# Transforms once per two steps, the first image's load in two parts, and ScalarE's second norm in another order, in a fused FFT-mixer and patch-attention kernel

## What is computed

```python
def block0(x):                       # channels 16, hidden 32
    h  = pw(ln(x), w_te)             # norm over channels, pointwise product
    F  = fft2(h, axes=(1, 2))
    fc = gelu(pw([real(F), imag(F)], w_fc))
    sp = real(ifft2(re + 1j * im))
    x1 = x + pw(sp, w_tp)
    h2 = pw(ln(x1), w_fe)            # the second norm
    d  = gelu(depthwise3x3(h2) + b_dw)
    return x1 + pw(d, w_fp)          # x2

def block1(x2):                      # hidden 192 = q, k, v of 64 each
    hidden = ln(x2) @ w_hidden       # the third norm
    q, k, v = split(conv3x3(hidden, w_qkv), 3)
    out = irfft2(rfft2(patches8x8(q)) * rfft2(patches8x8(k)))
    out = v * ln(out)                # norm over 64 channels
    return out @ w_out + x2
```

## Time and profile before

| what | us |
|---|---|
| runs | 236.47, 236.66, 239.24 (median 236.66) |
| the profiled execution | 237.58 |
| its span in the trace | 235.8 |
| busy in it: TensorE | 219.5 |
| busy in it: VectorE | 159.4 |
| busy in it: ScalarE | 133.8 |
| busy in it: GpSimd | 76.9 |

### The profile page before, as it was taken

How to read it: one execution, slowest core, us unless ns; L and a number is a source line. 1 busy time by engine, 2 the same in 40 slices (tenths; PEclk the granted TensorE clock), 3 DMA queues, 4 the chain that set the end, 5 groups by cost and what they waited for, 6 DMA issues and landing times.

```text
span 235.8 us, 4977 instructions
## 1 busy us (share of the span) xinstructions
PE 219.5 (93%) x1926; PEld 144.1 (61%) x1926; DVE 159.4 (68%) x301; ACT 133.8 (57%) x286; POOL 76.9 (33%) x70
## 2 busy tenths in 40 slices
PE   7989999895989899779999999999999999999983
PEld 3359434772447557268676676767676777767561
DVE  3995123567743983646489978678786889677793
ACT  3366475323174754344678666667667576766533
POOL 1635500012300000000051766426654364549730
PEclk9999999999799999999999999999999999999999
DMA  6920000000000018989997479999950000000001
GB/s 215 329 70 7 16 8 4 20 3 0 4 0 0 0 64 190 223 193 194 201 197 151 141 137 191 182 179 202 191 118 0 3 24 25 0 1 3 22 0 67
DMA packets 22647, 21.07 MB, mean 89 GB/s; under 512 B 1898, under 2 KB 21242, under 8 KB 22522
## 3 DMA queue, kind: packets, MB, share of 16 engines
q1 hardware_dynamic: 22352, 20.62, 43.0%
q10 hardware_dynamic: 272, 0.14, 0.3%
HBM read 16.58 MB, written 4.02 MB: 87 GB/s over the span
## 4 chain that ended last, share of the span: by engine, by line
PE 68%; DVE 16%; ACT 6%; DMA 6%; issue 2%; SPq 1%; DVEq 0%; ACTq 0%
PE psum L1229 22%; PE psum L1240 13%; PE psum L1250 7%; PE psum L1102 5%; PE psum L1175 4%; PE psum L1260 3%; DMA arena<-parts 3%; DVE xc L781 2%; PE psum L1080 2%; DVE sq L793 2%; PE psum L1090 2%; PE psum L1063 2%; DMA parts<-tr 2%; DVE st L787 2%; PE psum L1286 2%
## 5 line engine op out<-in xcount | busy, mean ns | idle before, releaser
L1229 PE MATMUL psum<-wc,tile 128*128 128x192 f32 (+1 forms) x384 | 59.4, 305 | 3.5 <-ACT tile L378 1.9
L1229 PEld LDWEIGHTS psum<-wc,tile 128*128 128x128 f32 (+1 forms) x384 | 51.4, 159 | 13.7 <-issue 7.8
L557 POOL TENSOR_TENSOR zp<-zp,ln 128x512 f32<-128x512 f32 x14 | 17.8, 1274 | 100.6 <-DVE zp L937 100.6
L916 DVE TENSOR_TENSOR arena<-psum,arena 128x512 f32<-128x512 f32 x32 | 22.1, 691 | 27.5 <-ACT arena L716 27.2
L378 DVE COPY tile<-arena 128x256 f32<-128x256 f32 x64 | 25.1, 435 | 2.1 <-DMA arena<-parts 2.1
L1175 PE MATMUL psum<-arena,wdw 102*128 102x512 f32 x48 | 23.5, 631 | 0.9 <-ACT arena L339 0.9
L716 ACT COPY arena<-psum 128x512 f32<-128x512 f32 x32 | 18.8, 586 | 9.0 <-PE psum L1240 9.0
L1250 PE MATMUL psum<-arena,km 128*64 128x256 f32 x128 | 20.9, 405 | 0.2 <-DVE arena L916 0.2
L709 ACT COPY spec<-psum 128x768 f32<-128x768 f32 x16 | 12.8, 799 | 12.7 <-PE psum L1229 12.7
L558 POOL TENSOR_TENSOR zp<-zp,ln 128x512 f32<-128x512 f32 x14 | 17.8, 1271 | 1.1
L1240 PE MATMUL psum<-spec,km 64*128 64x256 f32 x128 | 18.2, 402 | 0.0
(11 more groups left out here) (129 smaller groups left out, 373.1 us busy)
## 6 DMA issues: line engine op xcount, KB each, us to landing
arena<-padded SPq DMA_DIRECT2D x16, 393.0 KB, 9.8
arena<-parts SPq DMA_DIRECT2D x16, 196.5 KB, 9.7
arena<-padded SPq DMA_DIRECT2D x8, 262.0 KB, 10.4
parts<-tr SPq DMA_DIRECT2D x12, 115.5 KB
wq<-w_qkv SPq DMA_DIRECT2D x1, 1296.0 KB, 11.9
padded<-tr SPq DMA_DIRECT2D x4, 264.0 KB, 3.9
arena<-parts SPq DMA_DIRECT2D x8, 131.0 KB, 9.6
out<-xt SPq DMA_DIRECT2D x8, 128.0 KB, 1.7
```

The lines of the kernel that those rows point to most:

```text
L557: pool_link(pool.tensor_tensor(y, y, along(0), ALU.mult))
L916: dve.tensor_tensor(pr[:, m % 2], f_half(m, 0), kh[:, m % 2], ALU.mult).then_inc(prod, 1)
L1229: last = mm(bank[a][:, HID * h:HID * h + HID], stationary[:, n % 2, 2 * h + a, :], moving[:, :], start=first and h == 0, stop=not first, s ...
```

## The change

Three parts.

**ScalarE's second norm.** In group 0 the root of the first half (`deviation`) now comes before the square of the second half. In group 1 each window copy is followed by one square, both roots and the Gelu table come next, and the last two window copies stand behind the table. The rows are ScalarE's, from the copies of the inverse transform (line 652 before, 664 now) to the first Gelus (line 677 before, 692 now). Lines 588 and 593 are the square and the root before, 593 and 598 now; 339 is the window copy and 582, now 587, the table. Before:

The diff's core:

```diff
+            if n == 0:
+                engine.wait_ge(im_first, 16 * CHUNK_LOADS)
+            elif n == 2:
+                engine.wait_ge(im_ld[0][0], 16 * CHUNK_LOADS)
...
-            store_padded(0)
+            for b in range(2):
+                store_padded(b)
             store_parts(0)
-            load_chunk(0, 0, 0)
-            store_padded(1)
-            store_parts(1)
+            for p, done in enumerate((im_first, im_ld[0][0])):
+                load_taps(0, 2 * p, 2 * p + 2, done)
+                load_last(0, 2 * p, 2 * p + 2, done)
             sp_.wait_ge(fp_mm, 8)
...
+            deviation(1, 0, (0,))
             square(1, 0, (1,))
-            deviation(1, 0)
+            deviation(1, 0, (1,))
...
+                        store_parts(0, LANES[1:])
+                    if j == 7:
+                        store_parts(1, LANES)
...
-            for n in range(32):
+            for s in range(16):
+                gather9(2 * s + 1)
+                if s >= 2:
+                    o_square(s - 2)
+                conv_out(2 * s)
+                if s == 0:
+                    deviation(2, 1)
+                if s >= 1:
+                    k_out(s - 1)
+                if s in (1, 2):
+                    for b2 in range(2):
+                        part(1, s - 1, b2)
+                if s < 15:
+                    gather9(2 * s + 2)
+                if s >= 2:
+                    root(s - 2)
+                u = unit_after(s - 4)
+                if u is not None:
+                    unit_out(u)
+                conv_out(2 * s + 1)
+                if 3 <= s < 15:
+                    turned(s - 3)
...
+            def product(i):
+                dve.wait_ge(k_ev, i + 1)
+                dve.wait_ge(f_mm, i + 1)
+                if i >= 1:
+                    dve.wait_ge(o_mm, i)
+                dve.tensor_tensor(pr, psum[:, 1024:2048], kh, ALU.mult).then_inc(prod, 1)
...
+            for s in range(16):
+                gather(2 * s + 1)
+                if s == 1:
+                    bordered(1)
+                if s >= 2:
+                    o_sum(s - 2)
+                    o_centre(s - 2)
+                if s == 0:
+                    variance(2, 1)
+                if s < 15:
+                    gather(2 * s + 2)
...
-            keep_warm(5, km, 2)
+            keep_warm(4, km, 2)
...
+            def forward(i):
+                pe.wait_ge(qkv_ev, 2 * i + 2)
+                pe.wait_ge(x2_done, 8)
+                if i >= 1:
+                    pe.wait_ge(prod, i)
+                for part, name, signal in ((1, "fk", fk_mm), (0, "fq", f_mm)):
...
+            for s in range(16):
+                conv(2 * s)
+                if s >= 1:
+                    forward(s - 1)
+                u = unit_after(s - 4)
+                if u is not None:
+                    unit(u)
+                if s == 1:
+                    channel_major(1)
+                conv(2 * s + 1)
+                if 3 <= s < 15:
+                    turn(s - 3)
+                if s >= 1:
+                    inverse(s - 1)
...
-            keep_warm(2, km, 3)
+            keep_warm(1, km, 3)
```

More of the change, by code:

```diff
@@ L685, in _ @@
                 square(2, g, (1,))
[L686 removed]
+                if g == 0:
+                    deviation(2, 0)
             def gather9(n):
@@ L1257, in turn @@
                     pe.wait_ge(yt_ev, i)
+                    if unit_after(i - 1) is not None:
+                        pe.wait_ge(pj_ev, unit_after(i - 1) + 1)
                 pe.wait_ge(gated, i + 1)
@@ L1287, in unit @@
                 last.then_inc(pj_mm, 1)
-            for n in range(32):
-                conv(n)
-                if n >= 1:
-                    forward(n - 1)
-                if n == 1:
-                    pe.wait_ge(x2_done, 8)
-                    channel_major(1)
-                if n >= 2:
-                    inverse(n - 2)
-                if n % 2 == 1 and 7 <= n < 31:
-                    turn((n - 7) // 2)
-                u = unit_after((n - 8) // 2)
-                if n % 2 == 0 and u is not None:
-                    unit(u)
-            forward(31)
+            for s in range(16):
+                conv(2 * s)
+                if s >= 1:
+                    forward(s - 1)
+                u = unit_after(s - 4)
+                if u is not None:
+                    unit(u)
+                if s == 1:
+                    channel_major(1)
+                conv(2 * s + 1)
+                if 3 <= s < 15:
+                    turn(s - 3)
+                if s >= 1:
+                    inverse(s - 1)
+            for e in range(2):
+                forward_half(e)
             turn(12)
-            inverse(30)
-            inverse(31)
+            for e in range(2):
+                inverse_half(e)
             turn(13)
```

178 lines of the change are left out of this document (86 added, 92 removed).

## The result

The changed kernel took 241.01 us in the median of four runs (239.38 to 242.86), beside 237.29 for the kernel before. The ratio is 1.016, with a 95% interval of 1.010 to 1.022. It is slower, clear of noise, though by less than the 2% from which the prediction counts a kernel as slower; 232.2 was forecast, and 228.5 to 239 as the range.

What follows compares the result with a forecast made beforehand. TensorE's work was taken to bound the loop, with DMA rates limiting the loads before it. Conv 4 at 110.95 plus the pairs gave loop end 215.1, 4.5 us saved: 232.2 from the 236.66 median, range 228.5 to 239.

Steps and rivals of the forecast that it cites:

- The ring in pairs with a finish: Loop: chain of waits from product to product, through finish and gather; 7.5 us a pair, under TensorE's 7.65.
- the likeliest case: Whole kernel: only the gather is held up by GpSimd's gate, not finish; 232.2 us, chance 0.45 with the no-gain norm rival.
- its two rivals: Loop: finish and gather held up by GpSimd together once (233.7 us, chance 0.23) or one after the other (239.2, 0.12).
- held up twice: Loop, five pairs with a finish: GpSimd delays finish, then the gather again; 9.2 us a turn, 239.2 in all, chance 0.12.
- pairs without a finish: Loop: the gather, held up beside GpSimd's product, makes the chain of waits 7.3 us, over TensorE's 7.0.
- TensorE's own terms: Loop: TensorE's work is forward 1.9, inverse 1.0, a pair 7.0 us, or 7.65 with a unit.
- landing + 2.75: Before conv 4: second chunk's landing at 108.2, then gather, product, inverse and 0.1; conv 4 at 110.95 us.
- 3.84 MB at 196 GB/s from 87: First loads: the bytes left up to the second chunk take 19.6 us from about 87 us on.
- small pieces: First loads: 260-byte pieces add 1.0 us to the second chunk's landing; as a dearer rival 234.3 us, chance 0.10.
- so much is just covered: Before the loop: ScalarE's six stores take 3.81 us, the Gelu ends at 91.4, TensorE reaches its last projection at 91.3.
- 1.9 us earlier: Second norm: ScalarE's new order takes 0.9 + 0.98 us off everything up to the third norm; bounds 0.9 to 2.2.
- Late next is TensorE's own depthwise product: Second norm: with the waits for ScalarE gone, TensorE's depthwise product would be the next late operation; no size given.

Runs made afterwards that it cites:

- e4: The changed kernel with finish moved ahead of the product and the next pair's first gather moved ahead of the scale; 233.57 us, ratio 0.9873.
- e9: The changed kernel, nothing moved, with GpSimd's three gate operations working on only 8 elements of a partition; 232.65 us, ratio 0.9807.
- e3: The changed kernel with finish moved one pair later, ahead of the product; 235.58 us, ratio 0.9864.
- e6: e4 with image 1's parts stored by SyncE behind the split first loads, instead of by ScalarE ahead of them; 234.08 us, ratio 0.9865.
- e1: The kernel before with only ScalarE's new order of the second norm; 237.84 us, ratio 1.0017.
- e8: e7 with GpSimd's addition in the second norm made to wait until VectorE has normalised; 230.57 us, ratio 0.9700.
- e7: e4 with the product of pair 0 put ahead of the gather of step 4 on VectorE; 231.47 us, ratio 0.9745.
- e5: e4 with the first image's first chunk loaded whole, as before the change; 237.73 us, ratio 1.0015.
- e11: e8 with ScalarE's six stores put behind its last Gelu; 232.75 us, ratio 0.9796.
- e10: e8 with image 1's parts stored by SyncE behind the split first loads; 231.27 us, ratio 0.9745.

## Why the prediction was wrong

The miss in the profiled execution is 242.86 - 233.1 = 9.8 us, and all of it is there at the loop's end: 224.9 (the last whole inverse, 223.83 + 1.08) against the 215.1 of the sum. It falls into three pieces.

**The ring in pairs with a finish, 4.6 us.** This is the step that failed, and with it the choice of the likeliest case. The prediction wrote that in pairs with a unit "finish covers 0.8 of the product's 1.3, and the gather waits 0.5: 7.5, under 7.65". It took finish as cover for the gather, while finish itself is held up. Measured are 0.82 us more for the addition and 1.07 for the gather, together 1.9 (the prediction put the line between its two rivals at 1.5), and 8.87 for the turn, not 7.5. The rival "held up twice" named this mechanism, this place and 9.2 us a turn, and gave 239.2; the runs without a fall of the clock took 239.4 and 240.1. That they are so near is in part luck: the rival charged 7 us for the ring, the trace has 4.6, and the late landing below, which it did not have, makes up for the rest. It had a chance of 0.12. The evidence that should have raised it was named beside it: in the earlier trace rows the second copy of a pair waits after the first has passed, so GpSimd does get in between two queued instructions. The hope that "work of VectorE that is queued in a row may keep its turn" had no row. The five turns at 8.87 make 5 x (8.87 - 7.65) = 6.1 us; seen at TensorE's inverses it is 5.0 (43.2 us for five pairs against 38.25), and the other pairs, 7.2 to 7.6 us each, give back some tenths. e9 shows the cause: without GpSimd's load in the same order, 7.6 us go. e3 and e4 show it from the other side.

In the pairs without a finish the prediction was right: 7.3 forecast, 7.25 measured. So were TensorE's own terms: forward 1.9 (1.92 from start to start), inverse 1.0 (1.01), 7.0 and 7.65 for a pair (7.02 and 7.59 in e4), and what lies behind the loop (16.1 us, 16.2 by the sum).

**Conv 4, 3.6 us.** The sum had conv 4 at landing + 2.75; it came at 111.83 + 2.69. That rule held (2.69 or 2.70 in e3, e4, e6 and e9 too). What failed is the landing: 111.83, not 108.2. Two steps of it were wrong. First, "3.84 MB at 196 GB/s from 87". From 87 to 93.7 us the changed kernel moved 159 GB/s, since SyncE's first bfloat16 loads wait for image 0's stores, and these took 5.81 us beside ScalarE's six instead of about 4.2. And up to the second chunk's landing the engines moved more than these bytes, since the next chunk's loads were already under way:

```profile
87.00:93.70 6.70, 6.15 (x36) 4.30 (x35) 2.54 (x6) 1.85 (x3) 0.00 (x0) 1.00 0.62 159
...
87.00:111.80 24.80, 20.27 (x112) 14.12 (x110) 11.12 (x25) 10.42 (x22) 0.00 (x0) 1.00 0.99 182
```

24.8 us at 182 GB/s are 4.5 MB, 0.67 MB more than I counted: 3.4 us of transfer at 196 GB/s, and 1.8 more for the lower rate. The trace of the kernel before had it too: 4.70 MB from 87 us to its second landing. The prediction had charged 1.0 us for small pieces, and that term measured nothing; 3.4 + 1.8 - 1.0 are 4.2, against the 3.6 that are missing. The other 0.6 are the 0.4 for the first landing, which no row shows, and a slip: 87 + 19.6 + 0.4 is 107.0, not 107.2. The lower rate isn't the order's alone: e3, the same up to there, moved 4.44 MB at 200 GB/s and landed at 109.24. So about 1.0 of the 3.6 us is in every profile of this order of the loads (109.2 at the earliest), and up to 2.6 are this execution's, their cause open. The first part came at 98.89 and not 95.1, mostly for the stores' sake: in e6, without them beside, it came at 95.11. And "so much is just covered" of ScalarE's stores was not: they took 4.95 us, not 3.81, and TensorE stood 0.55 us. Second, the start was not 1.9 us earlier. That term was the norm's. Of it e1 showed at most 1.5 from the start of the norm, since the VectorE product of the first half fell beside GpSimd's addition (0.8 us, which e8 gave back), and the window copies put behind the table made TensorE stand 0.92 us. "Late next is TensorE's own depthwise product" was wrong: late next were the copies. The profiled execution was another 0.8 us late from its first loads on (VectorE's first addition of the norm at 50.54, against 49.71).

**The clock, 1.6 us.** Conv 4 took 1.15 us more and the forward behind it 0.47. The prediction had no term for it, though it forecast the idle time of over 2 us that stood before it, as idle time that costs only itself.

How much each part does, by the ratios: the norm alone 1.002 (no difference that can be told), norm and loads 0.994, all of it with finish moved 0.986 (0.979 to 0.994), as it was written 1.016.

What stays open: why the second chunk landed anywhere from 109.2 to 111.8 us in kernels that are the same up to there (109.24 in e3, 109.66 in e9, 111.62 in e4), and with it how much of e7's gain is the order's; and what of the fall of the clock could be spared by other warming products, which wasn't tried.

## What to carry to other kernels

When a change puts VectorE work with SBUF operands right behind the instruction that starts GpSimd, count each such instruction as ending with a GpSimd instruction of its own (here 0.8 and 1.1 us more), not the group once. A ring of waits is priced with its instructions as they will be beside their new neighbours; where its sum lies close to the engine that should bound (here 7.3 and 7.5 against 7.0 and 7.65), the order inside the ring decides, and moving two instructions was worth 3%. And idle time in front of TensorE's dense work can cost twice: itself, and the clock behind it (1.6 us here and in e6, 2.6 in e5).

## What the runs showed of the hardware

VectorE's copies from SBUF to SBUF (gather) and its additions and products with two SBUF inputs wait until a GpSimd instruction that is under way ends, and end 0.15 to 0.54 us behind it: 0.43 becomes 1.25, 0.49 becomes 1.56, 0.69 becomes 1.47. Between two of them GpSimd gets its next instruction in, although both were queued (160.19 and 161.55 above). An instruction of VectorE that reads PSUM keeps its time beside GpSimd: the centring at 171.19 took 0.69 us, as always, in the middle of GpSimd's second product.

```profile
171.19 0.69 DVE L959 SCALAR_TENSOR_TENSOR zp<-stat,psum 128x512 f32<-128x512 f32 x1
```

```profile
170.41 1.27 POOL L563 TENSOR_TENSOR zp<-zp,ln 128x512 f32<-128x512 f32 x1
```

The Trainium skill, "SBUF — State Buffer", "SBUF: two separate sides", states an exclusive lock on the port pair that the two share, held by whichever starts first "for the whole instruction". The durations here agree with it, for each instruction by itself; e9 shows that GpSimd's work is the cause, and that it is this lock no run shows.

TensorE's clock fell to its lower level behind idle stretches of 6.4 us (e5), 4.3 us (e6) and 2.1 us (the changed kernel and e11), and in the profile of the kernel before behind one of 0.93 us with 0.61 us of work and another 0.92 in front of it; but not in e4's profile behind 2.6 us, nor in e10's behind 2.2. So the length of the last idle stretch alone doesn't tell. And the six stores of ScalarE's queue beside three of SyncE's stretched the last of the latter from between 3.7 and 4.2 us to between 5.2 and 6.0, and to 4.7 when they were issued behind the last Gelu (e11).
